# Matrix products of zeros in three rests of TensorE, in a six-stage transformer kernel on one Trainium2 core

## The reference, cut to what matters

```python
x = x + 0.5 * ffn(layernorm(x))      # W1, W3 to 1024, silu*lin, Hadamard transform, W2
x = x + state_space(layernorm(x))    # conv, softplus, a scan over 512 tokens, 16 states, W_out
x = x + 0.5 * ffn(layernorm(x))      # the same weights again
x = x + 0.5 * moe(layernorm(x))      # 8 experts of 176, best 2 of them, and a shared one
x = x + attention(layernorm(x))      # 16 heads of 16, causal, with a bias by distance
x = x + 0.5 * moe(layernorm(x))      # the same weights again
```

```python
m = jnp.mean(x, axis=axis, keepdims=True)
v = jnp.var(x, axis=axis, keepdims=True)
return (x - m) / jnp.sqrt(v + eps)
```

## Time and profile before

| | us |
|---|---|
| three runs | 864.78, 865.47, 860.62 (median 864.78) |
| the profiled execution | 861.2, its span 859.4 |
| TensorE busy in the span | 757.6 (88%), weight loads 525.6 |
| VectorE, ScalarE, GpSimd busy | 560.4, 407.3, 254.0 |
| mean granted clock of TensorE | 0.957 |

### The profile page before, as it was taken

One profiled execution on the slowest core, in us unless ns is written; L12 is line 12 of the kernel. 1 busy time (PEld: TensorE's weight loads), 2 busy tenths in 40 slices (PEclk: granted clock), 3 DMA queues, 4 the chain that ended last, 5 costly groups with the idle time before them and its releaser, 6 DMA issues.

```text
span 859.4 us, 10715 instructions
## 1 busy us (share of the span) xinstructions
PE 757.6 (88%) x3809; PEld 525.6 (61%) x3823; DVE 560.4 (65%) x984; ACT 407.3 (47%) x600; POOL 254.0 (30%) x189
## 2 busy tenths in 40 slices
PE   3998979978779799996999998997889998786997
PEld 3687555643326466675877776775447785444786
DVE  4434699999969999953345546357655646843543
ACT  3344797665456787731232334351475431373221
POOL 0000059975328787841993000001000010000000
PEclk9999999998988999997998999999999999997999
DMA  8300022221102222207001000033000241000000
GB/s 279 111 2 1 8 57 78 81 75 57 41 27 61 62 73 67 82 26 227 1 1 21 1 1 1 13 97 101 15 1 1 67 117 39 2 26 1 1 0 25
DMA packets 30591, 41.75 MB, mean 49 GB/s; under 512 B 3753, under 2 KB 19955, under 8 KB 30515
## 3 DMA queue, kind: packets, MB, share of 16 engines
q1 hardware_dynamic: 29290, 40.91, 16.3%
q10 hardware_dynamic: 1252, 0.19, 0.2%
HBM read 36.73 MB, written 4.26 MB: 48 GB/s over the span
## 4 chain that ended last, share of the span: by engine, by line
PE 38%; DVE 5%; ACT 3%; DMA 3%; SPq 2%; issue 1%; DVEq 0%; ACTq 0%
PE PS L494 27%; PE PS L1015 2%; PE PS L998 2%; PE PS L554 2%; ACT shared L1520 1%; PE PS L699 1%; DMA scratch_k<-shared 1%; SPq L2171 1%; DMA shared<-scratch_q 1%; PE PS L1049 1%; DVE route L1963 1%; DVE work_r L1685 1%; PE PS L504 1%; SPq L2154 1%; DMA shared<-route 1%
## 5 line engine op out<-in xcount | busy, mean ns | idle before, releaser
L2227 POOL TENSOR_TENSOR shared<-shared,route 128x1024 f32<-128x1024 f32 x64 | 151.6, 2372 | 78.6 <-DVE shared L1919 77.5
L494 PE MATMUL PS<-xnT,weights_r 128*128 128x256 f32 (+1 forms) x744 | 161.9, 366 | 5.4 <-DVE xnT L1661 3.0
L494 PE MATMUL PS<-xnT,work_r 128*128 128x512 f32 (+1 forms) x624 | 156.8, 402 | 0.0
L1919 DVE TENSOR_TENSOR_SCAN shared<-shared,PS 128x512 f32<-128x512 f32 x128 | 148.6, 1202 | 0.0
L494 PEld LDWEIGHTS PS<-xnT,weights_r 128*128 128x128 f32 x744 | 119.2, 194 | 40.8 <-issue 22.2
L494 PEld LDWEIGHTS PS<-xnT,work_r 128*128 128x128 f32 (+1 forms) x624 | 114.2, 188 | 28.7 <-issue 1.4
L812 PE MATMUL PS<-shared,cf 128*128 128x512 f32 x256 | 125.5, 614 | 0.0
L1678 DVE TENSOR_TENSOR gated<-gated,PS 128x512 f32<-128x512 f32 (+1 forms) x52 | 35.6, 685 | 107.8 <-ACT gated L1178 107.8
L1178 ACT ACTIVATE gated<-PS 128x512 f32<-128x512 f32 (+1 forms) x52 | 31.0, 597 | 143.1 <-PE PS L494 138.5
L1462 ACT ACTIVATE shared<-shared,cols 128x512 f32<-128x512 f32 x128 | 83.6, 712 | 22.7 <-DVE shared L1919 18.8
L494 PE MATMUL PS<-weights_r,work_r 128*128 128x256 f32 (+1 forms) x624 | 89.0, 292 | 1.3 <-DVE work_r L1685 1.1
(11 more groups left out here) (208 smaller groups left out, 1063.3 us busy)
## 6 DMA issues: line engine op xcount, KB each, us to landing
route<-scratch_c SPq DMA_DIRECT2D x64, 256.0 KB, 3.2
shared<-in_L_ffn_W_dram SPq DMA_DIRECT2D x3, 1024.0 KB, 8.9
scratch_k<-shared SPq DMA_DIRECT2D x12, 128.0 KB
scratch_q<-shared SPq DMA_DIRECT2D x12, 128.0 KB
shared<-scratch_k SPq DMA_DIRECT2D x8, 192.0 KB
shared<-scratch_q SPq DMA_DIRECT2D x8, 192.0 KB
mamba_w<-in_L_ffn_w_dram SPq DMA_DIRECT2D x2, 704.0 KB, 5.4
beside<-in_L_ffn_w_dram SPq DMA_DIRECT2D x2, 704.0 KB, 7.5
```

The costliest lines, as they stand in the source:

```text
L494: last = nc.tensor.matmul(o, lhs[l], rhs[r], start=(start and i == 0), stop=(stop and i == 2))
L1919: v.tensor_tensor_scan(hst[:, (t % 2 * 2 + j) * T:(t % 2 * 2 + j + 1) * T], decay[t % D_SLOTS][:, j * T:(j + 1) * T], products[:, j * T:(j ...
L2227: nc.gpsimd.tensor_tensor(hc[:, u * 2 * T:(u + 1) * 2 * T].rearrange("p (c t) -> p c t", c=2), hst[:, (t % 2) * 2 * T:(t % 2 + 1) * 2 * T] ...
```

## The change

A method is added that issues a number of products of zeros into one bank, with no wait and no semaphore, and is called in the three rests, each time ahead of the transposes that wait for `xn_tok`: 8 products in rest 1 into bank 0, 13 in rest 2 into bank 0, 18 in rest 3 into bank 4. Nothing reads what they write.

```diff
+START_PRODUCTS, TAIL_PRODUCTS = 8, (13, 18)
...
+            def idle_products(self, at, count):
+
+                for _ in range(count):
+                    nc.tensor.matmul(bank(at), ident_b[:, :], zero_b[:, :], start=True, stop=True)
...
                     for n in range(4):
                         self.side_piece(0, n)
+                    self.idle_products(B_BANK, START_PRODUCTS)
                     for ch in range(DC):
                         self.norm_transpose(it + 1, ch, at=2 + ch)
...
                     pieces(PIECES - 2, PIECES)
+                    self.idle_products(B_BANK, TAIL_PRODUCTS[0])
                     for ch in range(DC):
                         self.norm_transpose(it + 3, ch, at=4 + ch)
...
                 project(1, 1).then_inc(down_done, 1)
+                if b == 1:
+                    self.idle_products(4, TAIL_PRODUCTS[1])
```

## The result

The changed kernel takes 857.72 us, median of 8 runs (854.90 to 860.57). The kernel before, in 8 runs with the three shown earlier among them, takes 865.46 (860.62 to 866.51). The ratio is 0.992, with a 95% interval from 0.9904 to 0.9936, so it is faster by 5.5 to 8.3 us (the medians differ by 7.7). The forecast was 858.2. Of all executions in this document one, of e8_over, was slow, with 1267.6 us at a mean granted clock of 0.556, for a reason that nothing here shows, and no ratio counts it.

The account below looks back on a forecast made before the run. TensorE, busy 757.6 of 859.4 us and at times at half clock, was taken as the bound. Gains of 1.0 + 3.2 + 0.65 = 4.85 us off 863.0 gave 858.2, range 854.3 to 863.3.

Parts of the forecast that it names:

- The price and cover of the products: Products in the rests take 0.215 us each and end 0.9, 0.9 and 1.6 us before `xn_tok`, so delay nothing.
- Rival D: Products run at half clock, outlast the rests and delay the transposes: 4.5 us slower, 867.5; chance 0.06.
- Rest 1: TensorE's wait ending at 79.19 us: the input product behind it starts at 82.0, not about 83.0; gain 1.0 us.
- Rests 2 and 3: TensorE's waits ending at 393.64 and 783.03 us: if the clock stays at 1.00, gains of 3.2 and 3.15 us.
- I let the clock hold in 1 and 2 and fall behind the transposes of rest 3: Full gains counted for the first two rests, 1.0 and 3.2 us, but only 0.65 for the third.
- the 0.65: Gain left in rest 3 if the clock falls behind its transposes; ends 0 and 3.15 us.
- stay at half speed as now: Router's and first expert's passes behind rest 3 remain at half clock, so their possible 2.5 us is not gained.
- the 0.66: Rest 2: full-clock transposes bring the first copy and last remainder sooner, `ffn` starts at 396.36; gain 0.66 us.
- A: Clock holds in all three rests: gain 7.35 us, 855.7; chance 0.18.
- B: Clock falls in what is left of rests 2 and 3, only the transposes gain: 2.3 us, 860.7; chance 0.20.
- How transposes count: Transposes seem to count as work for the clock, by trace rows against the skill's rule; otherwise the sum is B's.
- Does it reach the end: Shifts reach the kernel's end; bounds: all of the sum, or nothing of rests 1 and 2.

Follow-up runs that it names:

- e8_over: The changed kernel with 36 products instead of 18 in rest 3, more than the rest holds; 859.7 us, ratio 0.9938.
- e2_rest2: The changed kernel with only the 13 products of rest 2, those of rests 1 and 3 left out; 864.08 us, ratio 0.9996.
- e3_rest3: The changed kernel with only the 18 products of rest 3, those of rests 1 and 2 left out; 862.66 us, ratio 0.9977.
- e4_fill: The changed kernel with 7 more products behind the transposes of rests 2 and 3, 8 more ahead of rest 2's second feed-forward step; 855.14 us, ratio 0.9895.
- e7: The changed kernel with its products made of resident fp32r weights instead of the bf16 identity and zeros; 858.48 us, ratio 0.9898.
- e10: The changed kernel with 28 products of zeros added into an open sum in steps 25 to 29 of the first scan; 860.72 us, ratio 0.9930.
- e6: The changed kernel with 8 more products, only ahead of the second feed-forward step in rest 2; 857.59 us, ratio 0.9891.
- e5: The changed kernel with 7 more products, only behind the transposes of rest 2; 859.27 us, ratio 0.9907.
- e9: e4_fill with 7 and 3 more products in the first expert stage's two batches, where TensorE waits for routing weights; 852.65 us, ratio 0.9845.
- e11: All added products together: the three rests, their holes, the routing holes and the first scan's last steps; 850.60 us, ratio 0.9837 to before.
- e12: e4_fill unchanged, measured again on another chip; 852.86 us, ratio 0.9878 to before.

## Why the prediction was right, and where it was not

That the median came within half a microsecond of the forecast is luck: two errors met. The gain was put at 4.85 us and measures 6.9 (5.5 to 8.3). The level it was taken from, 863.0, the mean of four executions, was too low: the median of before is 865.46 in 8 runs and 865.45 in 29.

**The price and cover of the products: right.** They stand 0.215 us apart, end ahead of `xn_tok` in each rest with 0.82, 0.86 and 1.57 us left (forecast 0.9, 0.9, 1.6), and delay nothing. Rival D is out: in the changed kernel's profile no product ran at half speed. Its price for overrun was measured in e8_over.

**Rest 1: right in its own term.** 1.0 to 1.1 us up to the norm in the first scan. What it missed is that a shift moves everything behind it against the falls: 2.1 us more from there to the norm in the second scan. Before, e2_rest2 and e3_rest3, which all lack rest 1's products, take 90.1, 90.7 and 90.3 us there. Ten kernels with them take 87.4 to 88.7, and e4_fill, where the fall came at the chain's head as before, 89.6. So the place of the fall makes the difference, and not the products themselves.

**Rests 2 and 3: the full gains right, the choice and the size of a fall wrong.** The first step that failed is "I let the clock hold in 1 and 2 and fall behind the transposes of rest 3". In the changed kernel's profile it was the other way about. Over all profiles that have the products and open holes behind them, neither place is settled:

| | before | products, clock fell | products, clock held | first hole filled |
|---|---|---|---|---|
| rest 2 to next norm | 39.4 | 39.4 (changed), 39.1 (e2), 39.3 (e7), 39.3 (e10) | 36.2 (e8), 36.2 (e6) | 36.2 (e4, e5, e9, e11, e12) |
| rest 3 to the end | 76.4 | 75.7 (e5), 76.0 (e6), 76.0 (e10) | 72.9 (changed), 72.9 (e8) | 72.9 (e4, e11, e12) |

e3_rest3, e7_data and e9_route_hole, at 74.4 to 74.5, kept the clock behind rest 3 and lost it once in the passes from 800 us on. Where the clock holds, the worked-out sizes of 3.2 and 3.15 are the gaps of the table (3.2 and 3.4).

Where it falls, the sizes are wrong. In rest 3 the 0.65 seems to come out (0.4 to 0.7), but by luck. The prediction let the passes "stay at half speed as now", from 782.1 to 792.3. These are their rows in e10_steps, with the twelve passes of before as the last line:

```profile
782.69 1.09 PE L505 MATMUL PS<-cf,xn_tok 128*128 128x128 f32 x8 [1.56 <-DVE xn_tok L1665]
785.36 2.68 PE L495 MATMUL PS<-xnT,gateT 128*8 128x512 f32 x6 [1.57 <-DVE xnT L1675]
787.84 3.41 PE L495 MATMUL PS<-xnT,work_r 128*128 128x512 f32 x12
```

```profile
788.94 4.50 PE L494 MATMUL PS<-xnT,work_r 128*128 128x512 f32 x12
```

Here the clock is at 0.50 only from 785.5 to 788.9, and the twelve passes take 3.41 us and not 4.50. A second fall at 805.9 takes back what that spared. e5 and e6 show the same pair of falls, at 784.5 and 805.0 and at 782.9 and 803.4. In rest 2 a fall behind the transposes leaves nothing of the 0.66, because a second one follows at 400. The prediction had neither second fall. So A and B are not rival kernels but different executions of much the same kernel: with the products and an open first hole, the clock held in 2 of 6 profiles in rest 2 and in 4 of 7 in rest 3.

**How transposes count: open.** In rest 3 of the changed kernel 4.2 us pass between the end of the products of zeros and the first pass (780.75 to 784.99), with 1.09 us of transposes as the only work, and the clock stays at 1.00. But e6 and e10, with the same code there, lost it 2.6 and 2.8 us behind the first transpose. The Trainium skill (TensorE: Matmul & The Clock Gate, Part 4: PE-mode transpose) has it that transpose mode does not count as busy in the same way; the falls in e6 and e10 are what that rule would give, and the changed kernel's profile shows the clock held all the same. How much a transpose counts was not measured by itself, so the prediction's choice of the row over the rule is neither confirmed nor refuted.

**Does it reach the end: mostly.** Rest 3 does whole. Of what stood at rest 2, 3.0 us were lost up to the end of the first attention in that profile, which has falls at 529.6 and 615 where before has none. No edit touches that part, and it takes 109.7 to 112.7 us in the fourteen profiles; the part from there to rest 3, which only e8_over's overrun touches, takes 140.2 to 144.9. It looks like the same effect as in the scan, with the other sign, though no wait was traced there. Such parts are large enough to make single profiles differ by several us.

## What to carry to other kernels

Where TensorE rests for another engine and its next work finds the clock at half, unread products that end inside the rest delayed nothing here and, where the clock held, gave that work its full speed. Fill the small holes behind the rest too, up to where dense work starts: in rest 2 the rest alone left the clock to chance (36.2 us in 2 of 6 profiles), and with the first hole filled all five profiles had the 3.2 us. By time, the kernels with filled holes alone (0.9895 and 0.9878) are not clearly told from the changed one (0.992); only e9_route_hole and e11_all, with more places, are. One profile of a kernel whose clock falls is one draw: compare stretches between fixed points over several profiles before calling a microsecond the work of an edit.

## What the runs showed of the hardware

The granted clock stayed up on products of zeros as on products of weights (e7_data). That fall near 191 us is not spread at random over executions: it comes 123.6 to 124.8 us behind the transposes near 68 in all fourteen profiles, so a shift of one microsecond in between can decide which work the next falls hit. And a fall costs what the work that it slows is worth to others: 1.65 us at the head of a chain for which VectorE waits, nearly nothing one step earlier, where TensorE has 2.1 us of idle in each step.
